# The rotary pair sums of a linear-attention kernel: from accumulating DMAs to GpSimd adds and doubled TensorE products

## What is computed

```python
q = gelu(x @ Wq + bq) + 0.21
k = gelu(x @ Wk + bk) + 0.21
v = x @ Wv + bv
q_r = rope(q)                     # x * cos + xr * sin, xr = (-x1, x0) for each pair (x0, x1) of channels
k_r = rope(k)
# 16 heads of 16 channels
kmean = jnp.mean(k, axis=2, keepdims=True)
z = 1.0 / (einsum('bhnd,bhmd->bhnm', q, kmean) + 1e-06)
kv = einsum('bhnd,bhne->bhde', k_r, v) / n
out = einsum('bhnd,bhde->bhne', q_r, kv) * z
return layernorm(out + x, g, bb)
```

## Time and profile before

| | |
|---|---|
| median of 3 runs | 1808.33 us (1807.36 to 1809.34) |
| the profiled execution, its own time | 1807.36 us |
| its span in the trace | 1805.5 us |
| busy of the span | PE 98%, DVE 80%, ACT 51%, POOL 52% |
| granted TensorE clock, mean | 0.993 of full |
| attention stage | about 158 to 959 us |

### The profile page before, as it was taken

The page is one execution under the profiler, slowest core; times in us unless marked ns, Lnnn a source line. Parts: engine busy times, 40 slices in busy tenths (PEclk is TensorE's granted clock), DMA queues, the critical chain, the costliest instruction groups (busy, mean ns, idle before and its releaser), DMA issues.

```text
span 1805.5 us, 41765 instructions
## 1 busy us (share of the span) xinstructions
PE 1771.3 (98%) x17084; PEld 1437.2 (80%) x17084; DVE 1451.8 (80%) x3422; ACT 922.3 (51%) x1741; POOL 945.8 (52%) x743
## 2 busy tenths in 40 slices
PE   9999999999999999999998999999999999999998
PEld 3336788888888888888886988888888888888887
DVE  3667888889888889888887749697978788888887
ACT  4554667777766777766776723323333333232231
POOL 1556798888898888888881012131312121212221
PEclk9999999999999999999998999999999999999999
DMA  7364564454447644445458711010101010101000
GB/s 284 148 258 162 149 171 95 83 119 89 113 95 199 180 115 95 112 90 134 108 123 277 250 62 47 24 47 24 48 24 47 24 44 27 36 36 36 27 9 24
DMA packets 34800, 182.14 MB, mean 101 GB/s; under 512 B 6000, under 2 KB 6832, under 8 KB 21296
## 3 DMA queue, kind: packets, MB, share of 16 engines
q0 software_dynamic: 10880, 79.70, 20.6%
q1 hardware_dynamic: 20960, 89.62, 13.8%
q10 hardware_dynamic: 2768, 10.15, 1.5%
HBM read 80.89 MB, written 31.46 MB: 62 GB/s over the span
## 4 chain that ended last, share of the span: by engine, by line
PE 53%; POOL 36%; issue 6%; DVE 3%; DMA 1%; ACT 1%; ACTq 0%; SPq 0%; POOLq 0%; DVEq 0%
PE bankC L1431 13%; POOL yB L789 8%; POOL yB L792 8%; POOL qs L800 7%; PE bankC L32 7%; PE bankC L33 7%; PE bankC L34 7%; PE bankC L1430 6%; POOL qc L799 6%; PE hid_ps L245 3%; PE conv_ps L256 3%; POOL rstdB L815 3%; POOL qc L807 3%; POOL kr L773 2%; PE turn L1405 1%
## 5 line engine op out<-in xcount | busy, mean ns | idle before, releaser
L1431 PE MATMUL bankC<-down,act_hi 128*128 128x512 f32 x992 | 353.1, 397 | 0.0
L1430 PE MATMUL bankC<-down,act_lo 128*128 128x256 f32 x868 | 246.1, 284 | 0.0
L1431 PEld LDWEIGHTS bankC<-down,act_hi 128*128 128x128 f32 x992 | 186.4, 188 | 41.9
L1556 DVE TENSOR_TENSOR act_lo<-gel,act_hi 128x512 fp32r<-128x512 f32 x256 | 210.6, 822 | 8.7
L33 PE MATMUL bankC<-aT_lo,up_hi 128*128 128x512 f32 x512 | 199.6, 390 | 0.0
L32 PE MATMUL bankC<-aT_hi,up_hi 128*128 128x512 f32 x512 | 199.5, 390 | 0.0
L34 PE MATMUL bankC<-aT_hi,up_lo 128*128 128x512 f32 x512 | 199.4, 389 | 0.0
L1510 POOL TENSOR_TENSOR hC<-hC,vecC 128x1024 f32<-128x1024 f32 x16 | 38.6, 2414 | 283.9 <-PE turn L1405 283.9
L1516 POOL TENSOR_TENSOR rstdC<-var_epsC,minus_halfC 128x4 f32<-128x4 f32 x47 | 56.1, 1194 | 248.9 <-DVE var_epsC L1584 248.9
L1430 PEld LDWEIGHTS bankC<-down,act_lo 128*128 128x128 f32 x868 | 164.0, 189 | 1.4
L1473 ACT ACTIVATE aT_hi<-turn 128x512 fp32r<-128x512 f32 x64 | 34.8, 596 | 234.8 <-PE turn L1405 234.8
(11 more groups left out here) (211 smaller groups left out, 5171.8 us busy)
## 6 DMA issues: line engine op xcount, KB each, us to landing
kr<-kc POOLq DMA_DIRECT2D x32, 1024.0 KB, 7.0
qc<-qs POOLq DMA_DIRECT2D x64, 512.0 KB, 6.7
raw_late<-in_AB SPq DMA_DIRECT2D x30, 320.0 KB, 3.8
u<-hA SPq DMA_DIRECT2D x8, 1024.0 KB, 4.9
u_next<-u SPq DMA_DIRECT2D x8, 1024.0 KB, 5.1
hC<-u SPq DMA_DIRECT2D x16, 512.0 KB, 4.1
xC<-in_x SPq DMA_DIRECT2D x16, 512.0 KB, 4.9
out<-w_flat SPq DMA_DIRECT2D x15, 512.0 KB, 2.6
```

The costliest lines, as they stand in the source:

```text
L1430: e.matmul(bank[:, 0:H], a_lo[:, fb, tok], both[k][:, fb, 0, :], start=False, stop=False)
L1431: m = e.matmul(bank[:, :], a_hi[:, fb, tok], both[k][:, fb, :, :].rearrange("p a h -> p (a h)"), start=fb == 0, stop=fb == FB - 1)
L1556: e.tensor_tensor(a_lo[:, fb, :], g, a_hi[:, fb, :].bitcast(F32), ALU.subtract).then_inc(s_act_lo, 1)
```

## The change

The three accumulating DMAs of a unit go. For k, GpSimd adds `kc` onto `kr` itself, in four operations of 128x512, one for each quarter as it becomes ready. For q, the sum is not formed at all: since q_r = qc + R·qs with a fixed matrix R that swaps neighbours and signs one of them, the product with `kv` is the sum of qc by `kv` and qs by R-transposed·`kv`. A new matmul `turn_kv` multiplies the 128x64 tile `kv` by the constant `rot`, VectorE copies the result to `kv_rot` (`copy_turned`), and `outputs` makes two accumulating sets of 32 matmuls in place of one. On GpSimd `invert(n-2)` moves from the end of the round to the place behind `residual(n)`. A 64 KB load of `rot` is added to the tables, and the sign in the sine table of q goes.

```diff
-            def sum_k(n):
-                w.wait_ge(s_ks, 4 * n + 4)
-                e.dma_start(flat(kr), flat(kc), accum_op=ALU.add).then_inc(d_kr, 16)
+            def sum_k(n, u):
+                w.wait_ge(s_ks, 4 * n + u + 1)
+                e.tensor_tensor(kr[:, u, :], kr[:, u, :], kc[:, u, :], ALU.add).then_inc(s_kr, 1)
...
-            def sum_q(n):
-
-                w.wait_ge(s_qr, 3 * n + 3)
-                w.wait_ge(s_qd, n + 1)
-                for a in range(2):
-                    e.dma_start(flat(qc)[a::2, :], flat(qs)[1 - a::2, :], accum_op=ALU.add).then_inc(d_qr, 16)
-
...
-                if n < 2:
+                if n >= 2:
+                    invert(n - 2)
+                else:
                     for g in (2 * n, 2 * n + 1):
                         conv.last.gpsimd(e, w, g)
-                sum_k(n)
+                for u in range(DUOS):
+                    sum_k(n, u)
                 for x, db in ((0, 0), (0, 1), (1, 0)):
                     rotate_q(n, x, db)
-                sum_q(n)
-                if n >= 2:
-                    invert(n - 2)
...
-                        w.wait_ge(d_kr, 16 * (n + 1))
+                        w.wait_ge(s_kr, 4 * n + u + 1)
...
+            def turn_kv(n):
+                w.wait_ge(d_consts, 3 * 16)
+                w.wait_ge(s_kvw, n + 1)
+
+                if n + 1 < UNITS:
+                    w.wait_ge(s_lo, 4 * (n + 1) + 2)
+                else:
+                    w.wait_ge(s_vs, 4 * n + 4)
+                e.matmul(big[0][:, 0:CB * D], rot[:, :], kv[:, :, :].rearrange("p c n -> p (c n)"),
+                         start=True, stop=True).then_inc(s_rot, 1)
+
             def outputs(n):
-                w.wait_ge(d_qr, 2 * 16 * (n + 1))
-                w.wait_ge(s_kvw, n + 1)
+                w.wait_ge(s_qr, 3 * n + 3)
+                w.wait_ge(s_qd, n + 1)
+                w.wait_ge(s_kvr, n + 1)
...
                 for db in range(CB):
-                    for j in range(QUARTERS):
-                        for i in range(GR):
-                            ch = slice(D * i, D * i + D)
-                            out = big[i][D * j:D * j + D, :].rearrange("p (a d c) -> p a d c", a=TILES, d=CB)[:, :, db, :]
-                            m = e.matmul(out, kv[ch, db, :], quarter(qc[ch, db, :], j), start=True, stop=True)
+                    for wt, q in ((kv, qc), (kv_rot, qs)):
+                        for j in range(QUARTERS):
+                            for i in range(GR):
+                                ch = slice(D * i, D * i + D)
+                                out = big[i][D * j:D * j + D, :].rearrange("p (a d c) -> p a d c", a=TILES, d=CB)[:, :, db, :]
+                                m = e.matmul(out, wt[ch, db, :], quarter(q[ch, db, :], j), start=q is qc, stop=q is qs)
...
+                if n >= 1:
+                    turn_kv(n - 1)
                 turn_k(n, 0)
...
+            turn_kv(UNITS - 1)
             outputs(UNITS - 1)
...
+            def copy_turned(n):
+                w.wait_ge(s_rot, n + 1)
+                w.wait_ge(s_out, n)
+                e.tensor_copy(kv_rot[:, :, :].rearrange("p c n -> p (c n)"),
+                              big[0][:, 0:CB * D]).then_inc(s_kvr, 1)
```

More of the change, by code:

```diff
@@ L639, in attention_phase @@
         y_rows = [place[f"yB{s}"] for s in range(LANES)]
-        kr, qc, qs, gT, v, gain, shift, kv_mask, mean_mask = (
-            place[n] for n in ("kr", "qc", "qs", "gT", "v", "gain", "shift", "kv_mask", "mean_mask"))
+        kr, qc, qs, gT, v, gain, shift, rot, kv_mask, mean_mask = (
+            place[n] for n in ("kr", "qc", "qs", "gT", "v", "gain", "shift", "rot", "kv_mask", "mean_mask"))
         w_all = [keep["w_first"], keep["w_second"]]
@@ L672, in attention_phase @@
         s_memset, s_hT, s_hi, s_lo, s_mul, s_res = (sem(n) for n in ("memset", "hT", "hi", "lo", "mul", "res"))
-        s_k, s_gk, s_kt, s_ks, d_kr, d_qr = (sem(n) for n in ("k", "gk", "kt", "ks", "d_kr", "d_qr"))
+        s_k, s_gk, s_kt, s_ks, s_kr = (sem(n) for n in ("k", "gk", "kt", "ks", "kr"))
         s_q, s_gelu, s_gq, s_qr, s_qd, s_v, s_vs = (sem(n) for n in ("q", "gelu", "gq", "qr", "qd", "v", "vs"))
         s_ksum, s_km, s_den, s_dens, s_dent, s_z = (sem(n) for n in ("ksum", "km", "den", "dens", "dent", "z"))
-        s_kv, s_kvm, s_kvw = (sem(n) for n in ("kv", "kvm", "kvw"))
+        s_kv, s_kvm, s_kvw, s_rot, s_kvr = (sem(n) for n in ("kv", "kvm", "kvw", "rot", "kvr"))
         s_out, s_turned, s_scaled, s_y = (sem(n) for n in ("out", "turned", "scaled", "y"))
@@ L1164, in vector @@
                     measure(n - 2, 1)
+                if n >= 1:
+                    copy_turned(n - 1)
                 if n == 0:
@@ L1184, in vector @@
             key_value(UNITS - 1)
+            copy_turned(UNITS - 1)
             def last(k):
@@ L1195, in vector @@
             then(e, last)
-        free = {"hT": [(s_v, 4 * UNITS)], "gkT, kc": [(s_kt, 4 * UNITS), (d_kr, 16 * UNITS)],
-                "tables of q": [(s_qr, 3 * UNITS), (s_qd, UNITS)], "ring": [(s_kvw, UNITS)], "masks": [(s_kvw, UNITS), (s_km, UNITS)], "big": [(s_y, 4 * UNITS)],
+        free = {"hT": [(s_v, 4 * UNITS)], "gkT, kc": [(s_kt, 4 * UNITS), (s_kr, 4 * UNITS)],
+                "tables of q": [(s_qr, 3 * UNITS), (s_qd, UNITS)], "ring": [(s_kvr, UNITS)], "big": [(s_y, 4 * UNITS)],
                 "all": [(s_unit, 8 * UNITS)] + [(d, 16 * (B // 2)) for d in d_sent]}
@@ L1742, in gpsimd @@
             last(0)
-            wait_free(Waits(e), before.free["masks"])
+            wait_free(Waits(e), before.free["ring"])
             e.memset(zero[:, :].bitcast(F32), 0.0).then_inc(s_zero, 1)
@@ L1889, in build @@
         under(ctx, [("w_first", weights, F32R)], [("w_flat", [P, 4 * 3 * H])])
-        under(ctx, [("kv_mask", [P, CB, 32]), ("mean_mask", [P, CB, 32])], [("zero", [P, 512], F32R)])
+        under(ctx, [("rot", [P, P]), ("kv_mask", [P, CB, 32]), ("mean_mask", [P, CB, 32])], [("zero", [P, 512], F32R)])
         under(ctx, [("raw_late", [P, 3, width])], [("act1_hi", [P, 8, 512], F32R)], [("cos_k", rows), ("sin_k", rows)])
@@ L1927, in load_tables @@
             e.dma_start(flat(place["shift"]), t["shift_rows"].partition_broadcast(P)).then_inc(keep["d_rows"], 16)
+            e.dma_start(place["rot"][:, :], t["rot"]).then_inc(keep["d_masks"], 16)
             e.dma_start(flat(place["kv_mask"]), t["kv_mask"]).then_inc(keep["d_masks"], 16)
@@ L2033, in layout @@
     d["cos_k"], d["sin_k"] = rows(cos), rows(sin * sign)
-    d["cos_q"], d["sin_q"] = cols(cos), cols(-sin * sign)
+    d["cos_q"], d["sin_q"] = cols(cos), cols(sin)
+    i = np.arange(0, 128, 2)
+    rot = np.zeros((128, 128), np.float32)
+    rot[i + 1, i], rot[i, i + 1] = 1, -1
+    d["rot"] = rot
     p = np.arange(128)
```

7 lines of the change are left out of this document (4 added, 3 removed).

## The result

The kernel after took 1832.45 us (median of 4 runs, 1831.74 to 1833.35) beside 1808.84 us (4 runs, 1807.36 to 1813.73) of the kernel before: 1.013 times as long, interval 1.011 to 1.0145. Its profiled execution took 1829.56 us with a span of 1827.8.

The account below looks back on a forecast made before the run. TensorE's own work was taken to set the 24.4 us attention round. From the profiled 1807.36 us: +45.6 over 31 rounds, -2 waits, +7.2 first unit, -6 stage end, giving 1852 us, range 1834 to 1868.

Parts of the forecast that it names:

- f: First unit: GpSimd's longer row holds VectorE's L135, +5.5 us, plus a low clock, +1.7: together +7.2 us (-5 to +15).
- The +1.7 for a low clock in unit 1: Unit 1: after TensorE idles over 10 us, its product passes run at the 1.2 GHz level, +1.7 us.
- a + b + c: Each attention round: TensorE's added work less what waits give back, +1.47 us (0.9 to 2.0), +45.6 us over 31 rounds.
- a: `outputs` in each round: the second set of 32 matmuls costs +1.43 us (1.1 to 1.49).
- b: `turn_kv` in each round: one float32 matmul in two records, +0.24 us (0.1 to 0.5).
- c: Each round: TensorE's gaps ahead of the fourth q product and `values` go, -0.2 us (-0.3 to 0); `copy_turned` is covered.
- e: DMA waits inside the attention stage, where `outputs` and `key_value` stood waiting, go: -2 us (0 to -4).
- d: GpSimd's round: loses 4.73 us, gains four adds of 5.0 us, becomes 24.8 us, has 1.1 to spare and costs nothing.
- the rival GpSimd: Attention rounds: slower adds make GpSimd the bound at 26.8 us a round, 1881 us in all; chance 0.06.
- The copy held up: Rival in the rounds: GpSimd shuts out `copy_turned` as it did L135, +7 us a round, 2025 us; chance 0.03.
- g: End of the attention stage: the last `outputs` no longer waits 8.43 us for the q DMAs, -6 us.

## Why the prediction was wrong

**The step that failed is f, the first unit**: +7.2 us forecast, -5.8 measured, 13 of the 22.5 us by which the account missed. I read L135's 7.73 us as a hold by GpSimd's six operations, and carried it over to a row of ten. The row that stood ahead of them, the DMA L773 at 174.65, I passed by, although the change removes exactly that. With the DMA back the hold is back (7.72 us), with one more it is 22.02 us, and with no DMA ahead L135 waits for one operation at most. The trace of the kernel before had this contrast in it, 11 us earlier: there L135 came up in the midst of GpSimd's row of four 128x1024 operations, with no DMA ahead of them, and was done in 0.44 us, when the operation then running was over. Timelines of POOL and DVE before:

```profile
162.47 4.76 POOL L792 TENSOR_TENSOR yB<-yB,shift 128x1024 f32<-128x1024 f32 x2
```
```profile
164.48 0.44 DVE L135 TENSOR_SCALAR minus_meanA<-momentsA 128x4 f32<-128x4 f32 x1
```

The lower end of f, -5, "if VectorE gets in already between two adds", was the true case. The rule of the Trainium skill that I set aside (SBUF — State Buffer, section "Who interferes with whom"), by which VectorE waits for one GpSimd operation, gave f as near -5. It agrees with the rows without a DMA ahead (0.48 us); it does not agree with those behind one (7.7 and 22 us). Rule and row were both right, each for its own case, and going by the row was wrong because I did not ask what was special about it. The +1.7 for a low clock in unit 1 fell with the idle time.

**a + b + c, the stack of a round**: forecast +1.47, measured +1.19, 8.4 us over 30 rounds. Mis-sized were a (1.43 forecast, 1.26 measured: the drain at the end of `outputs`, about 0.16 us, is paid once; it was the choice between 1.1 and 1.49 that I made too high), b (0.24; 0.16) and c (-0.20; the products for q and v, 72 records, fell from 11.65 to 11.31 us, -0.34). Not foreseen was +0.10 in `key_value`: with four waits for the adds in place of one for the DMA it took 1.33 us and not 1.24, and 1.24 again in the run with the k DMA back. The sum 1.26 + 0.16 - 0.34 + 0.10 is 1.18. The mechanism, TensorE pays, is borne out by the run without the second set; there a and the -0.34 go together, 0.91 us a round.

**e, waits given back**: -2 forecast, +3.8 measured. The waits for DMAs went, but stalls inside `outputs` came: what the 30 rounds take above clean ones added up to 4.75 us before and 8.55 after. This miss of 5.8 us went the other way; without this luck the time would have lain some 6 us further below the range.

**d and the rival GpSimd**: right. It waits 1.71 us a round (about 1 forecast), and the adds start 1.25 us apart. The rival was near: without the q part GpSimd was the bound, at 1858 us.

**The copy held up**: did not happen, 0.23 us with no delay. In the kernel after it never comes up behind a GpSimd DMA, so no run shows what one would do to it; L1137, which also reads PSUM, took 0.10 us right behind one.

**g, the end**: right in kind and nearly in size, -5.5 against -4.5. The clock stayed up, and with the slow start of the feed-forward products, which gave back 0.95 us within their first six, it is -6.5.

**Not in the sum: the closing of the program.** Of the 3.9 us that the feed-forward part gained, 2.56 lie behind the last matmul, where GpSimd's DRAIN no longer sets the end. I had put this stretch at nothing without looking at it. It is not what differs from run to run: the eight traces without q DMAs have 5.8 to 5.9 us there, the six with them 7.9 to 8.5. The last 0.40 us stay open.

**Not in the sum: the start.** The 2.05 us lie in the convolution stage. The granted clock was 0.50 from 16 to 18 us before and 1.00 after. The run without the second set, with the same convolutions as after, had 0.50 there too and reached the first product for k at 158.52 us, as before. So this differs from run to run and is no effect of the change.

Together: -12.98 - 8.40 + 5.80 - 1.94 - 2.05 - 2.96 = -22.53 us, and 1852.13 (the forecast before rounding) less 22.53 is 1829.60, which is the profiled execution's 1829.56 but for rounding. The range was narrower than its own terms: their low end gave 1830, and I took only the inner part, from 1834.

## What to carry to other kernels

When a small operation shows a duration many times its own, look not only at what runs beside it but at what stood just ahead of that, and ask whether the change removes it. A change that costs a little in every round and gains at both ends can be kept at the ends alone: that made 1797 us, where the kernel before takes 1809 to 1813 and the kernel after 1832. And two halves of a change may each be bad alone (1846 and 1858 us) for different reasons, so the sum of single effects is no guide to the whole.

## What the runs showed of the hardware

- A DMA issued by GpSimd, of 1 MB or 128 KB, adding or copying, kept VectorE's 128x4 `tensor_scalar` from SBUF to SBUF out for 22 us, until GpSimd's row of operations came to a wait. In each case the operation had come up while the row of the DMA was running. With no DMA of GpSimd's ahead it took 0.48 us, the rest of one GpSimd operation; so too with the same copy issued by SyncE, which had landed by then.
- Behind an accumulating DMA of its own, GpSimd's operations read 0.2 to 0.6 us longer (128x512: 1.58 for 1.29; 128x1024: 2.95 to 2.99 for 2.39 to 2.41; the 128x8 pow: 2.2 for 1.66). The starts of the large ones lay as far apart as ever; only behind the small one was time lost.
- A set of 32 matmuls on 32x32 tiles (64 records) took 1.43 us alone and 1.26 us more when it ran on from another.
- GpSimd's closing DRAIN took 1.43 us in kernels where GpSimd issues 8 DMAs in all, 1.51 with 9, 4.04 with 40, 6.17 with 98, 6.54 with 104, and 6.65 with 72 (64 of them q DMAs). What else it depends on isn't shown.
